# Short node tile moved as 112 rows and one, chunk bounds by TensorE transposes, pair table only in the general path, ScalarE normalises four tiles

## The chip, the cores and the metric

One core of one Trainium2 chip runs the whole program. The metric is the device time of one execution in microseconds, lower is better; the number to forecast is the median of the runs of the changed kernel.

## The reference

Two graph blocks over 625 nodes of 1024 features and 20,000 edges, each followed by a residual and a layer norm. Per edge there are `src`, `dst` (sorted) and a type of 2 and one of 8.

```python
x = _layernorm(x + _L0_gnn_ref(x, edge_index, edge_type_2, ...), axis=-1)
x = _layernorm(x + _L1_gnn_ref(x, edge_index, edge_type_8, ...), axis=-1)
# L0: norm_x = ln_weight * x * rsqrt(mean(x^2) + 1e-6)
#     y = elu(norm_x @ W_root + bias + sum_r mean over edges of type r of (norm_x[src] @ W_rel[r]))
#     returns x + y @ wo_weight
# L1: u = x @ root + bias + sum_r mean_r(x[src]) @ weight[r]          (8 types)
#     z = concat([u, x]) @ w_gate + b_gate;  returns tanh(u) * z + x * (1 - z)
```

## The kernel before

The program is written by hand for each engine (`block.sync`, `gpsimd`, `scalar`, `tensor`, `vector`), and semaphores order the engines among each other: each engine runs its own list from top to bottom, and a wait holds back all that stands behind it. Nodes lie on partitions in NT = 5 tiles of 128 rows; the last has TAIL = 113 real rows and 15 of zeros.

**Loading.** SyncE (SP) issues all DMAs. It loads the four edge lists, the norm weight, four full tiles of x in one DMA (L384) and, after the zeros are in place (`x_padded`), the 113 rows (L386). `x_loaded` of 32 means both have landed. It releases ScalarE's first work, the squares of `x` (L496), and SP's loads of the first weights (L396).

**Edge windows.** The mean over edges is done by matmuls with count matrices. The edges lie in 160 chunks of 125; nodes in 45 windows of 14 (`NWIN`). For each window VectorE finds the chunks that touch it, makes one-hot matrices of five chunks (`onehot_few`, L1319 and L1322), TensorE multiplies them (`count_few`, L837) and ScalarE copies the counts out (`copy_few`, L572 and L573). If a window ever needs more than MEET = 5 chunks, all three engines take a general path (`onehot_any` and its partners), which needs a table of pairs; with these inputs the short path runs. Which chunks touch a window comes from a bound for each of 80 partitions (L1209 to L1214), the maximum over the partitions by GpSimd (`partition_all_reduce`, L472, semaphore `bounds_max`), and a chain of twelve small VectorE instructions (L1225 to L1237) that makes the table and `most`, the largest number of chunks. All engines wait for that (`table_ready`).

**Order of VectorE in the first stage.** Windows 0 and 1, then the reciprocal of the RMS deviation (L1366, waits for ScalarE's `std`, L499), windows 2 and 3, splits of the transposed x (L1245), windows to 8, then the scale of the first weights, which waits for GpSimd's second `partition_all_reduce` (L482). That one waits for the absolute sums of the weights by ScalarE (`w0_sums`, L607). ScalarE normalises x (L611, `norm_x`) and TensorE transposes it (L826, `turn`) in between.

**GpSimd.** It clears x's last tile, makes the identity matrix (`ident`: a memset and an affine_select, L447 to L449) and the index constants (`consts_ready`, 12 in all), then runs the reductions above and one for each later weight unit.

**The last stage.** For tile t VectorE takes tanh(u) minus x, and for each half adds the gate product (L1760), multiplies (L1762), adds to x (L1763) and takes statistics (L1473). After the first half of tile t it normalises tile t - 1 in place (`norm_apply`: a reciprocal, L1481, and the 128x1024 subtract and multiply, L1485); ScalarE gives the deviation (L688), and SP stores tile t - 1 (L440). The last tile is normalised at the very end and its 113 rows are stored. SP then waits for all stores (L84).

```python
sp.wait_ge(x_padded, 1)
sp.dma_start(x[0:TAIL, NT - 1, :], x_d[(NT - 1) * P:NODES, :]).then_inc(x_loaded, 16)

pool.wait_ge(bounds_ready, 1)
nc.gpsimd.partition_all_reduce(wtmp[:, 10:12, :]..., wtmp[:, 8:10, :]..., CP, RMAX).then_inc(bounds_max, 1)

pool.wait_ge(w0_sums, DC)
pool.sem_inc(pool_turns, 1)
nc.gpsimd.partition_all_reduce(ar0[:, :], am0[:, :], P, RMAX).then_inc(max_ready, 1)
```

Of the kernel before, what the change touches and what calls it, by code (L numbers as in the profile page):

```python
# [5 lines left out]
ALU = mybir.AluOpType  # L6
ACT = mybir.ActivationFunctionType
AX = mybir.AxisListType
# [8 lines left out]
NPAD = NT * P  # L17
TAIL = NODES - (NT - 1) * P
DC = D // P
HALF = D // 2  # L20
# [61 lines left out]
def build(nc, x_d, src_d, dst_d, t2_d, t8_d, lnw_d, wrel_d, wroot_d, cb_d, wo_d,  # L82
          w1_d, root_d, b1_d, wg_d, bg_d, out_d):
    with ExitStack() as ctx:  # L84
        def sb(name, shape, dt):
            return ctx.enter_context(nc.sbuf_tensor(name, shape, dt))
# [4 lines left out]
        def sem(name):  # L91
            return ctx.enter_context(nc.semaphore(name))
# [18 lines left out]
        table = sb("table", [1, NWIN, 5], I32)  # L111

        most = sb("most", [1, 1], I32)
        rcnt0 = sb("rcnt0", [P, R0, NT], F32)
# [97 lines left out]
        keyT_ready = sem("keyT_ready")  # L212
        bounds_ready = sem("bounds_ready")
        bounds_max = sem("bounds_max")
        table_ready = sem("table_ready")
        onehot_free = sem("onehot_free")
# [78 lines left out]
        z_done = sem("z_done")  # L295
        out_ready = sem("out_ready")
        out_stored = sem("out_stored")

# [81 lines left out]
        def _(sp):  # L380
# [4 lines left out]
            sp.wait_ge(x_padded, 1)  # L385
            sp.dma_start(x[0:TAIL, NT - 1, :], x_d[(NT - 1) * P:NODES, :]).then_inc(x_loaded, 16)  # L386

# [3 lines left out]
            st0 = unit_weights(U_W0)[0]  # L391
            sp.wait_ge(x_loaded, 32)
            for a in range(2):
# [41 lines left out]
            for t in range(NT):  # L435
                sp.dma_start(x[:, t, :], x1_home[:, t, :]).then_inc(x1_back, 16)
            for t in range(NT):
                n = P if t < NT - 1 else TAIL
                sp.wait_ge(out_ready, t + 1)
                sp.dma_start(out_d[t * P:t * P + n, :], x[0:n, t, :]).then_inc(out_stored, 16)  # L440
            sp.wait_ge(out_stored, 16 * NT)


        @block.gpsimd
        def _(pool):
            nc.gpsimd.memset(x[:, NT - 1, :], 0.0).then_inc(x_padded, 1)
            nc.gpsimd.memset(ident[:, :], 0.0).then_inc(pool_steps, 1)  # L447
# [22 lines left out]

            pool.wait_ge(bounds_ready, 1)
            nc.gpsimd.partition_all_reduce(wtmp[:, 10:12, :].rearrange("p a j -> p (a j)"),  # L472
                                           wtmp[:, 8:10, :].rearrange("p a j -> p (a j)"), CP, RMAX).then_inc(bounds_max, 1)

            def unit_max(i, slot, parts=4):
# [16 lines left out]
        def _(act):  # L492
            act.wait_ge(x_loaded, 32)

# [90 lines left out]
            def copy_windows(j0, j1):  # L585

                with act.If(most_chunks <= MEET):
                    by_twos(act, j0, j1, copy_few)
                with act.Else():
                    by_twos(act, j0, j1, copy_any)  # L590

# [94 lines left out]
            def ln_deviation(k, t):  # L686
                act.wait_ge(ln_var[k], t + 1)
                nc.scalar.activation(std[:, 1 + k, t:t + 1], mv[:, k, t, 1:2], ACT.Sqrt, bias=eps[:, 1:2]).then_inc(ln_std[k], 1)  # L688
# [112 lines left out]
            for t in range(NT):  # L801
                if t + 2 < NT:
                    split_hi(2, t + 2, uT, 1.0)
                ln_deviation(1, t)


        @block.tensor
        def _(pe):
# [6 lines left out]
            last = nc.tensor.transpose(psC[:, 3 * CH:3 * CH + DC], lnw[:, :], ident[0:DC, 0:DC])  # L815
            last.then_inc(keys_turned, 1)

            def turn(k, t, src, ready):
# [43 lines left out]
            def count_windows(j0, j1):  # L862

                with pe.If(most_chunks <= MEET):
                    by_twos(pe, j0, j1, count_few)
                with pe.Else():
                    by_twos(pe, j0, j1, count_any)

# [299 lines left out]
        def _(dve):  # L1168
# [26 lines left out]


            dve.wait_ge(edges_loaded, 64)
            nc.vector.tensor_copy(ekey[:, 0, :, :], edges[:, 0, :, :]).then_inc(keys_ready, 1)
# [6 lines left out]
            step(ts(ctmp[:, 5, :], ctmp[:, 3, :], 16.0, None, ALU.mult))  # L1205
            dve.wait_ge(consts_ready, 12)
            base = win_base[0:CP, :]
            for h in range(2):
                step(ts(wtmp[:, h, :], base, ctmp[:, 5, h:h + 1], None, ALU.is_le))  # L1209
                step(stt(wtmp[:, 2 + h, :], base, ctmp[:, 4, h:h + 1], wtmp[:, h, :], ALU.is_ge, ALU.mult))  # L1210
                step(ts(wtmp[:, 4 + h, :], wtmp[:, 2 + h, :], ctmp[:, 0, h:h + 1], None, ALU.mult))
                step(ts(wtmp[:, 6 + h, :], wtmp[:, 2 + h, :], ctmp[:, 1, h:h + 1], None, ALU.mult))
            step(tt(wtmp[:, 8, :], wtmp[:, 4, :], wtmp[:, 5, :], ALU.max))
            tt(wtmp[:, 9, :], wtmp[:, 6, :], wtmp[:, 7, :], ALU.max).then_inc(bounds_ready, 1)  # L1214
            dve.wait_ge(keys_turned, 1)
# [3 lines left out]


            dve.wait_ge(bounds_max, 1)

            def row(a):
                return wtmp[0:1, a, :]
            step(ts(row(12), row(10), -1.0, 200.0, ALU.mult, ALU.add))  # L1225
            step(tt(row(13), row(11), row(12), ALU.subtract))
            pairs_i = wtmp[0:1, 14, :].bitcast(I32)
            step(ts(pairs_i, row(13), 0.5, 0.25, ALU.mult, ALU.add))
            step(ts(row(15), pairs_i, float(PAIRS), None, ALU.max))
            step(ts(row(16), row(15), -2.0, float(CH), ALU.mult, ALU.add))  # L1230
            step(nc.vector.tensor_tensor_scan(row(17), row(22), row(15), 0.0, ALU.mult, ALU.add))
            step(tt(table[:, :, 0], row(12), row(16), ALU.min))
            step(nc.vector.tensor_copy(table[:, :, 1], row(15)))
            step(tt(table[:, :, 2], row(17), row(15), ALU.subtract))
            step(nc.vector.tensor_copy(table[:, :, 3], row(17)))
            step(ts(table[:, :, 4], row(12), float(CH - MEET), None, ALU.min))
            nc.vector.tensor_reduce(most[:, :], row(13), AX.X, ALU.max).then_inc(table_ready, 1)  # L1237

            def split_lo(k, t, dst, gain):
# [67 lines left out]
            dve.wait_ge(table_ready, 1)  # L1307
            dve.wait_ge(keyT_ready, 1)
            most_chunks = dve.value_load(most[0:1, 0:1], min_val=1, max_val=CH)
            win8 = iota_win[0:EC, 0:WIN * R1]  # L1310
# [32 lines left out]
            def onehot_windows(j0, j1):  # L1343

                with dve.If(most_chunks <= MEET):
                    by_twos(dve, j0, j1, onehot_few)
                with dve.Else():
                    by_twos(dve, j0, j1, onehot_any)

# [400 lines left out]
            for t in range(NT):  # L1750
# [4 lines left out]
                for h in range(2):  # L1755
# [9 lines left out]
                    if t and h == 0:  # L1765
                        norm_apply(1, t - 1, out_ready)
                norm_var(1, t)
            norm_apply(1, NT - 1, out_ready)

# [22 lines left out]
```

## Time and profile before

| what | value |
|---|---|
| time, median of 3 runs (lowest to highest) | 974.63 us (973.67 to 975.96) |
| profiled execution, its own time | 975.7 us |
| its span | 973.8 us |
| TensorE busy / VectorE / ScalarE / GpSimd | 886.3 / 738.9 / 458.6 / 20.5 us |
| DMA | 63.43 MB, mean 65 GB/s |
| granted TensorE clock, mean | 0.97 |

The profile's page divides the span into 40 slices of 24.3 us. TensorE is busy for nine tenths of most slices from the fourth to the thirty-ninth; the first two and the last are the ones with room. The DMA engines move little after the start: the third slice has 3 GB/s and the second 178. The views used below are the timeline (start, duration, engine, line, operation, and in square brackets how long the engine was idle before it and what ended that), the chain of waits that ended last, busy time by stretch, the waits of SP, and the list of DMA issues.

### The profile page before, as it was taken

To read this page: it belongs to the slowest core of one execution; us is meant where nothing else is said; L and a number is where in the kernel's file an instruction comes from. 1 tells how busy PE (TensorE), PEld (TensorE's weight loads), DVE (VectorE), ACT (ScalarE), POOL (GpSimd) and SP (SyncE) were. 2 spreads that over 40 slices of the span, in tenths; PEclk is the share of its full clock that TensorE was granted. 3 is DMA by queue.
4 is the path that set the end of the run, shared out by engine and by line. 5 is a ranking of instruction groups with operands and counts; after the bars stand their busy time and mean duration, and the time that the engine had idled before them with its cause. 6 is when DMAs were issued, how large, how long until landed. Compare 5 with 4: busy or idle time off the path is not lost.

```text
span 973.8 us, 18919 instructions
## 1 busy us (share of the span) xinstructions
PE 886.3 (91%) x7115; PEld 648.0 (67%) x7116; DVE 738.9 (76%) x1216; ACT 458.6 (47%) x748; POOL 20.5 (2%) x46
## 2 busy tenths in 40 slices
PE   0568999898999899999999999999999999999980
PEld 0555887654458776787687787778778767876440
DVE  3589999496899777777777877776787777776891
ACT  0684445365465545535535453553544455338200
POOL 1000001000000000000000000000000000000000
PEclk9789999999999999999999999999999999999995
DMA  3501000251202222022022202202210220222011
GB/s 114 178 3 50 1 0 0 90 217 66 87 1 87 87 87 87 1 88 87 5 81 86 77 9 86 86 0 86 86 55 31 86 86 23 88 87 108 22 44 41
DMA packets 30343, 63.43 MB, mean 65 GB/s; under 512 B 1481, under 2 KB 4689, under 8 KB 30289
## 3 DMA queue, kind: packets, MB, share of 16 engines
q1 hardware_dynamic: 30289, 62.71, 18.2%
q8 instruction: 34, 0.56, 0.2%
q14 instruction: 20, 0.16, 0.1%
HBM read 57.52 MB, written 5.18 MB: 64 GB/s over the span
## 4 chain that ended last, share of the span: by engine, by line
PE 76%; DVE 12%; ACT 4%; DMA 3%; issue 2%; DVEq 0%; SPq 0%; POOL 0%; ACTq 0%; POOLq 0%
PE psP L1037 40%; PE psA L1107 18%; PE psP L837 6%; PE psP L886 4%; PE psA L875 4%; DMA x<-in_x 3%; DVE wsplit L1279 2%; PE psP L962 1%; DVE wsplit L1273 1%; PE psA L826 1%; DVE stats L1473 1%; DVE u_mem L1518 1%; DVE wsplit L1393 1%; ACT u_mem L607 1%; ACT wsplit L548 1%
## 5 line engine op out<-in xcount | busy, mean ns | idle before, releaser
L1037 PE MATMUL psP<-wsplit,xT 128*128 128x256 f16 x2592 | 296.4, 273 | 3.2 <-ACT vec L734 2.8
L1037 PEld LDWEIGHTS psP<-wsplit,xT 128*128 128x128 f16 x2592 | 254.3, 98 | 37.5 <-issue 3.1
L1107 PE MATMUL psA<-p_mem,c_mem 128*128 128x512 f16 x800 | 175.3, 379 | 0.0
L1037 PE MATMUL psP<-wsplit,x 128*128 128x256 f16 x1296 | 150.3, 273 | 1.7 <-DVE key_mem L1584 1.5
L1107 PEld LDWEIGHTS psA<-p_mem,c_mem 128*128 (+1 forms) x800 | 78.4, 98 | 90.9
L1037 PEld LDWEIGHTS psP<-wsplit,x 128*128 128x128 f16 x1296 | 126.6, 98 | 16.8 <-issue 2.2
L1279 DVE SCALAR_TENSOR_TENSOR wsplit<-stage,sc,wsplit 128x1024 f16<-128x1024 f32 x90 | 114.8, 1279 | 26.5 <-ACT wsplit L559 26.5
L559 ACT ACTIVATE wsplit<-stage,sc 128x1024 f16<-128x1024 f32 x90 | 100.6, 1137 | 15.0 <-DVE sc L1184 9.1
L837 PE MATMUL psP<-p_mem 125*128 125x140 f16 x1125 | 79.1, 234 | 22.7 <-DVE p_mem L1322 18.2
L837 PEld LDWEIGHTS psP<-p_mem 125*128 125x128 f16 x1125 | 76.2, 103 | 27.0 <-issue 14.9
L1549 DVE SCALAR_TENSOR_TENSOR u_mem<-psA,coef,u_mem 128x512 f32<-128x512 f32 x80 | 60.0, 750 | 32.9 <-PE psA L1107 30.9
L559 ACT ACTIVATE wsplit<-x,sc 128x1024 f16<-128x1024 f32 x54 | 61.7, 1143 | 39.2 <-PE psP L1037 32.6
L1279 DVE SCALAR_TENSOR_TENSOR wsplit<-x,sc,wsplit 128x1024 f16<-128x1024 f32 x54 | 69.2, 1282 | 10.3 <-ACT wsplit L559 10.2
L538 ACT ACTIVATE key_mem<-stage 128x1024 f16<-128x1024 f32 x72 | 75.8, 1053 | 1.7
L1322 DVE TENSOR_SCALAR p_mem<-iota_src,key_mem 125x640 f16<-125x640 f16 x225 | 70.4, 382 | 0.0
L572 ACT ACTIVATE c_mem<-psP 128x336 f32 (+1 forms) x90 | 36.8, 411 | 42.8 <-PE psP L837 42.8
L886 PE MATMUL psP<-wsplit,xT 128*128 128x512 f16 x240 | 54.3, 387 | 1.0 <-DVE u_mem L1518 1.0
L886 PE MATMUL psP<-wsplit,c_mem 128*128 128x512 f16 x240 | 52.5, 379 | 1.7 <-DVE wsplit L1273 1.7
L734 ACT ACTIVATE vec<-psP 128x512 f32<-128x512 f32 x16 | 9.5, 594 | 93.2 <-PE psP L1037 93.2
L1319 DVE SCALAR_TENSOR_TENSOR p_mem<-iota_win,win_base,key_mem 125x560 f16<-125x560 f16 x90 | 48.3, 579 | 5.7 <-issue 2.7
L875 PE MATMUL psA<-wsplit,xT 128*128 128x429 f16 x240 | 48.6, 353 | 3.5 <-issue 2.4
L1565 DVE SCALAR_TENSOR_TENSOR p_mem<-psP,p_mem 128x512 f16<-128x512 f32 x32 | 22.1, 692 | 32.2 <-ACT p_mem L731 32.2
(201 smaller groups left out, 804.8 us busy)
## 6 DMA issues: line engine op xcount, KB each, us to landing
stage<-in_L_gnn_weight SPq DMA_DIRECT2D x16, 2048.0 KB, 8.0
stage<-in_L_gnn_w_gate SPq DMA_DIRECT2D x4, 2048.0 KB, 7.9
x_home<-x SPq DMA_DIRECT2D x5, 512.0 KB, 2.6
x<-x_home SPq DMA_DIRECT2D x5, 512.0 KB, 5.5
stage<-in_L_gnn_W_rel SPq DMA_DIRECT2D x4, 572.0 KB, 8.6
x<-in_x SPq DMA_DIRECT2D x1, 2048.0 KB
xT<-in_L_gnn_root SPq DMA_DIRECT2D x1, 2048.0 KB, 7.9
stage<-in_L_gnn_root SPq DMA_DIRECT2D x1, 2048.0 KB, 8.1
```

Source lines behind the costliest of these rows:

```text
L538: nc.scalar.activation(land, st[:, part], ACT.Abs, accum_out=am[:, slot, n:n + 1]).then_inc(wsum_ready, 1)
L559: nc.scalar.activation(split_block(n, 0), step_block(REL, slot, n), ACT.Copy, scale=sc_f[:, scale_col(REL, slot), 2:3]).then_inc(whi_ready, 1)
L572: nc.scalar.activation(o8, w8, ACT.Copy)
L837: last = nc.tensor.matmul(psP[:, 2 * b + s // 3, col:col + WCOLS], src[:, s * P:(s + 1) * P], win, start=(first and s % 3 == 0), stop=Fals ...
L875: last = nc.tensor.matmul(out, lhs[:, a, c, bass.ts(t, P)], w[:, c, cols], start=first, stop=(c == chunks - 1 and a == 1))
L886: last = nc.tensor.matmul(out, lhs[:, a, c, bass.ts(t, P)], wsplit[:, s:s + 2, b, cols], start=first, stop=(c == DC - 1 and a == 1))
L1037: last = nc.tensor.matmul(psP[:, bank, (col + tt) * FB:(col + tt + 1) * FB], lhs[tt](a, c), split_block(n, b)[:, c, :], start=(first and t ...
L1107: last = nc.tensor.matmul(psA[:, (NT * h + t) % 2, :], cnt8[:, r, s, t * P:(t + 1) * P], p_part[h][a][:, s, :], start=(s == 0 and a == 0), ...
L1279: stt(split_block(n, 1), step_block(REL, slot, n), sc_f[:, scale_col(REL, slot), 2:3], split_block(n, 0), ALU.mult, ALU.subtract).then_inc ...
L1319: stt(oh_win[:, b, :, cols], w.unsqueeze(1).broadcast_to([EC, MEET, n]), wb, keyT[:, bass.ds(chunk, MEET), a:a + 1].broadcast_to([EC, MEET ...
L1322: ts(oh_src[:, b, k, :], iota_src[0:EC, :], keyT[:, chunk + k, 0:1], None, ALU.is_equal).then_inc(chunk_ready, 1)
L1549: stt(uv, psA[:, (NT * h + t) % 2, :], coef[:, t:t + 1], uv, ALU.mult, ALU.add).then_inc(agg_done, 1)
```

## The change

- The last tile of x is loaded, and stored, as two DMAs: rows 0 to 111 and row 112. `x_loaded` now counts to 48, and the last stores wait for a semaphore of their own, `last_ready`.
- The zeros of x's last tile are written by VectorE, no longer by GpSimd.
- The bounds are made by six instructions over both halves at once plus one maximum, behind four of the constants and not twelve. The maximum over partitions is a TensorE transpose, a VectorE maximum, and a second transpose; GpSimd's `partition_all_reduce` for it is gone.
- Of the twelve instructions of the table four remain (read straight from PSUM); the other eight are run only in the general path (`pair_table`).
- In the last stage ScalarE normalises tiles 0 to 3, with `shift` and `rstd` from VectorE; VectorE still does tile 4.

```diff
+EVEN = TAIL // 16 * 16
 # sync
-            sp.dma_start(x[0:TAIL, NT - 1, :], x_d[(NT - 1) * P:NODES, :]).then_inc(x_loaded, 16)
+            for r0, r1 in ((0, EVEN), (EVEN, TAIL)):
+                sp.dma_start(x[r0:r1, NT - 1, :], x_d[(NT - 1) * P + r0:(NT - 1) * P + r1, :]).then_inc(x_loaded, 16)
...
-            sp.wait_ge(x_loaded, 32)
+            sp.wait_ge(x_loaded, 48)
...
-            for t in range(NT):
-                n = P if t < NT - 1 else TAIL
+            for t in range(NT - 1):
                 sp.wait_ge(out_ready, t + 1)
-                sp.dma_start(out_d[t * P:t * P + n, :], x[0:n, t, :]).then_inc(out_stored, 16)
-            sp.wait_ge(out_stored, 16 * NT)
+                sp.dma_start(out_d[t * P:(t + 1) * P, :], x[:, t, :]).then_inc(out_stored, 16)
+            sp.wait_ge(last_ready, 1)
+            for r0, r1 in ((0, EVEN), (EVEN, TAIL)):
+                sp.dma_start(out_d[(NT - 1) * P + r0:(NT - 1) * P + r1, :], x[r0:r1, NT - 1, :]).then_inc(out_stored, 16)
+            sp.wait_ge(out_stored, 16 * (NT + 1))
 # gpsimd
-            nc.gpsimd.memset(x[:, NT - 1, :], 0.0).then_inc(x_padded, 1)
...
-            pool.wait_ge(bounds_ready, 1)
-            nc.gpsimd.partition_all_reduce(wtmp[:, 10:12, :].rearrange("p a j -> p (a j)"),
-                                           wtmp[:, 8:10, :].rearrange("p a j -> p (a j)"), CP, RMAX).then_inc(bounds_max, 1)
 # scalar, last stage, t from 0 to 4
+                if t:
+                    act.wait_ge(out_factors, 2 * t)
+                    nc.scalar.activation(x[:, t - 1, :], x[:, t - 1, :], ACT.Identity, bias=shift[:, t - 1:t],
+                                         scale=rstd[:, 2, t - 1:t]).then_inc(out_ready, 1)
                 ln_deviation(1, t)
 # tensor, behind the transposes of the keys
+            pe.wait_ge(bounds_ready, 1)
+            nc.tensor.transpose(psA[0:2 * NWIN, 0, 0:CP], wtmp[:, 8:10, :].rearrange("p a j -> p (a j)"),
+                                ident[0:CP, 0:CP]).then_inc(bounds_turned, 1)
+            pe.wait_ge(bounds_top, 1)
+            nc.tensor.transpose(psA[0:1, 1, 0:2 * NWIN], btop[:, :], ident[0:2 * NWIN, 0:2 * NWIN]).then_inc(bounds_max, 1)
 # vector
+            nc.vector.memset(x[:, NT - 1, :], 0.0).then_inc(x_padded, 1)
...
-            dve.wait_ge(consts_ready, 12)
-            base = win_base[0:CP, :]
-            for h in range(2):
-                step(ts(wtmp[:, h, :], base, ctmp[:, 5, h:h + 1], None, ALU.is_le))
...
+            dve.wait_ge(consts_ready, 4)
+            base = win_base[0:CP, :].unsqueeze(1).broadcast_to([CP, 2, NWIN])
...
+            step(tt(wtmp[:, 0:2, :], base, by_half(5), ALU.is_le))
...
+            tt(wtmp[:, 8:10, :], ends[:, 0, :, :], ends[:, 1, :, :], ALU.max).then_inc(bounds_ready, 1)
             dve.wait_ge(keys_turned, 1)
...
+            dve.wait_ge(bounds_turned, 1)
+            nc.vector.tensor_reduce(btop[:, :], psA[0:2 * NWIN, 0, 0:CP], AX.X, ALU.max).then_inc(bounds_top, 1)
             dve.wait_ge(bounds_max, 1)
...
+            low, high = psA[0:1, 1, 0:NWIN], psA[0:1, 1, NWIN:2 * NWIN]
+            step(ts(row(12), low, -1.0, 200.0, ALU.mult, ALU.add))
+            step(tt(row(13), high, row(12), ALU.subtract))
+            ts(table[:, :, 4], row(12), float(CH - MEET), None, ALU.min)
             nc.vector.tensor_reduce(most[:, :], row(13), AX.X, ALU.max).then_inc(table_ready, 1)
...
 # vector, last stage
                     if t and h == 0:
-                        norm_apply(1, t - 1, out_ready)
+                        norm_reciprocal(1, t - 1).then_inc(out_factors, 1)
+                        dve.wait_ge(out_factors, 2 * t - 1)
+                        ts(shift[:, t - 1:t], mv[:, 1, t - 1, 0:1], rstd[:, 2, t - 1:t], -1.0,
+                           ALU.mult, ALU.mult).then_inc(out_factors, 1)
                 norm_var(1, t)
-            norm_apply(1, NT - 1, out_ready)
+            norm_apply(1, NT - 1, last_ready)
```

The order of instructions is shown at two places. First GpSimd behind its constants, before the change (`ISA` is an instruction of GpSimd's own set; one with operands here is a `partition_all_reduce`, the bare one ahead of the first of them is added when the program is built):

```order
L468 MEMSET c_mem 128x40x10
L469 MEMSET u_mem 128x10x10
L472 ISA
L472 ISA u_mem<-u_mem 80x90 [waits bounds_ready]
L482 ISA ar<-am 128x8 [waits w0_sums]
```

and in the changed program:

```order
L477 MEMSET c_mem 128x40x10
L478 MEMSET u_mem 128x10x10
L487 ISA [waits w0_sums]
L487 ISA ar<-am 128x8
L489 MEMSET stage 128x1024 [waits w0_lo]
```

The reduction of the bounds is gone, and the bare instruction that stood in front of it, ahead of the wait for `bounds_ready`, now stands in front of the reduction of the weights' sums, behind the wait for `w0_sums`.

Second, VectorE in the last stage between the two halves of a tile, before:

```order
L1473 BN_STATS stats<-x 128x6 [waits dve_steps]
L1481 RECIPROCAL rstd<-std 128x1 [waits ln_var1,ln_std1,dve_steps]
L1485 TENSOR_SCALAR x<-x,mv,rstd 128x1024 [waits dve_steps]
L1760 SCALAR_TENSOR_TENSOR p_mem<-psP,cz,p_mem 128x512 [waits z_full]
L1762 TENSOR_TENSOR p_mem<-p_mem,u_mem 128x512 [waits z_done]
```

and now:

```order
L1508 BN_STATS stats<-x 128x6 [waits dve_steps]
L1516 RECIPROCAL rstd<-std 128x1 [waits ln_var1,ln_std1,dve_steps]
L1803 TENSOR_SCALAR shift<-mv,rstd 128x1 [waits out_factors]
L1795 SCALAR_TENSOR_TENSOR p_mem<-psP,cz,p_mem 128x512 [waits z_full]
L1797 TENSOR_TENSOR p_mem<-p_mem,u_mem 128x512 [waits z_done]
```

A 128x1024 instruction has given way to one of 128x1; the wide one stands on ScalarE, ahead of its deviation of the next tile.

## Rows read from the trace of the kernel before

**Rows 1.** The page: busy time, share of the span and instructions of each engine.
```profile
PE 886.3 (91%) x7115; PEld 648.0 (67%) x7116; DVE 738.9 (76%) x1216; ACT 458.6 (47%) x748; POOL 20.5 (2%) x46
```
**Rows 2.** The chain that ended last, start: start us, us, what.
```profile
3.53 25.02 DMA x<-in_x
```
**Rows 3.** Busy time by stretch: stretch, us, engines (instructions), clock, DMA share, GB/s.
```profile
6.00:10.00 4.00, 0.53 (x3) 0.53 (x3) 0.28 (x2) 0.00 (x0) 0.86 (x5) 1.00 1.02 412
10.30:28.40 18.10, 3.30 (x26) 3.09 (x26) 9.55 (x35) 0.00 (x0) 1.94 (x11) 1.00 0.06 26
```
**Rows 4.** Timeline, 0 to 36 us, all engines.
```profile
0.74 0.95 POOL L446 MEMSET x<- 128x1024 f32 x1 [0.29 <-POOLq L1782]
...
9.13 0.28 POOL L449 TENSOR_SCALAR_AFFINE_SELECT ident<-ident 128x128 f32<-128x128 f32 x1 [7.30 <-issue]
...
9.47 1.55 PE L813 MATMUL psC<-ident,u_mem 80*125 80x80 f32 x6 [9.47 <-POOL ident L449]
...
9.64 0.12 POOL L456 IOTA u_mem<- 80x2 f32 x1
...
11.43 0.17 POOL L469 MEMSET u_mem<- 128x100 f16 x1
...
13.91 0.20 DVE L1214 TENSOR_TENSOR u_mem<-u_mem 80x45 f32<-80x45 f32 x1
...
19.00 0.63 POOL L472 PARTITION_ALL_REDUCE u_mem<-u_mem  x1 [7.40 <-issue]
...
22.23 0.19 DVE L1237 TENSOR_REDUCE most<-u_mem 1x1 int32<-1x45 f32 x1
24.50 1.07 DVE L1319 SCALAR_TENSOR_TENSOR p_mem<-iota_win,win_base,key_mem 125x560 f16<-125x560 f16 x2 [2.08 <-issue]
...
26.02 5.50 PE L837 MATMUL psP<-p_mem 125*128 125x140 f16 x50 [14.80 <-DVE p_mem L1322]
...
28.58 1.06 ACT L496 ACTIVATE wsplit<-x 128x1024 f32<-128x1024 f32 x1 [26.55 <-DMA x<-in_x]
...
35.53 0.19 DVE L1366 RECIPROCAL rstd<-std 128x5 f32<-128x5 f32 x1 [6.00 <-ACT std L499]
```
**Rows 5.** Timeline, 36 to 75 us, TensorE, GpSimd and VectorE.
```profile
37.40 1.97 PE L826 MATMUL psA<-ident,wsplit 128*128 128x128 f32 x8 [5.89 <-ACT wsplit L611]
...
43.88 5.14 PE L837 MATMUL psP<-p_mem 125*128 125x140 f16 x50
...
48.86 1.04 PE L826 MATMUL psA<-ident,wsplit 128*128 128x128 f32 x8
...
64.55 1.18 POOL L482 PARTITION_ALL_REDUCE ar<-am  x1 [44.91 <-ACT u_mem L607]
...
68.75 1.08 DVE L1319 SCALAR_TENSOR_TENSOR p_mem<-iota_win,win_base,key_mem 125x560 f16<-125x560 f16 x2 [0.86 <-PE psP L837]
```
**Rows 6.** Timeline, 925 to 974 us, last stage.
```profile
925.64 20.88 PE L886 MATMUL psP<-wsplit,c_mem 128*128 128x512 f16 x96
...
931.46 0.16 DVE L1481 RECIPROCAL rstd<-std 128x1 f32<-128x1 f32 x1
...
932.39 0.75 DVE L1760 SCALAR_TENSOR_TENSOR p_mem<-psP,cz,p_mem 128x512 f32<-128x512 f32 x1
...
948.76 0.75 DVE L1760 SCALAR_TENSOR_TENSOR p_mem<-psP,cz,p_mem 128x512 f32<-128x512 f32 x1
...
952.49 0.81 DVE L1485 TENSOR_SCALAR x<-x,mv,rstd 128x1024 f32<-128x1024 f32 x1
```
**Rows 7.** Timeline, 210 us, VectorE, factors of the first layer norm.
```profile
210.13 0.16 DVE L1481 RECIPROCAL rstd<-std 128x1 f32<-128x1 f32 x1 [0.38 <-ACT std L688]
...
210.46 0.55 DVE L1454 TENSOR_TENSOR p_mem<-psA,p_mem 128x384 f16<-128x384 f32 x1
```
**Rows 8.** SP's waits (us in total, times, longest), and a DMA issue (KB, us to landing).
```profile
SPq L84 <- DMA out<-x: 19.8, 1, 19.8
...
x_home<-x SPq DMA_DIRECT2D x5, 512.0 KB, 2.6
```

More of the change, by code:

```diff
@@ L111, in build @@
         table = sb("table", [1, NWIN, 5], I32)
+        btop = sb("btop", [2 * NWIN, 1], F32)
         most = sb("most", [1, 1], I32)
@@ L213, in build @@
         bounds_ready = sem("bounds_ready")
+        bounds_turned = sem("bounds_turned")
+        bounds_top = sem("bounds_top")
         bounds_max = sem("bounds_max")
+        pairs_ready = sem("pairs_ready")
         table_ready = sem("table_ready")
@@ L296, in build @@
         out_ready = sem("out_ready")
+        out_factors = sem("out_factors")
+        last_ready = sem("last_ready")
         out_stored = sem("out_stored")
@@ L492, in _ @@
         def _(act):
-            act.wait_ge(x_loaded, 32)
+            act.wait_ge(x_loaded, 48)
             for t in range(NT):
@@ L589, in copy_windows @@
                 with act.Else():
+                    if j0 == 0:
+                        act.wait_ge(pairs_ready, 8)
                     by_twos(act, j0, j1, copy_any)
@@ L866, in count_windows @@
                 with pe.Else():
+                    if j0 == 0:
+                        pe.wait_ge(pairs_ready, 8)
                     by_twos(pe, j0, j1, count_any)
@@ L1205, in _, with by_half @@
             step(ts(ctmp[:, 5, :], ctmp[:, 3, :], 16.0, None, ALU.mult))
-            dve.wait_ge(consts_ready, 12)
-            base = win_base[0:CP, :]
-            for h in range(2):
-                step(ts(wtmp[:, h, :], base, ctmp[:, 5, h:h + 1], None, ALU.is_le))
[L1210 to L1214, printed above, removed]
+            dve.wait_ge(consts_ready, 4)
+            base = win_base[0:CP, :].unsqueeze(1).broadcast_to([CP, 2, NWIN])
+            def by_half(a):
+                return ctmp[:, a, :].unsqueeze(2).broadcast_to([CP, 2, NWIN])
+            step(tt(wtmp[:, 0:2, :], base, by_half(5), ALU.is_le))
+            step(tt(wtmp[:, 2:4, :], base, by_half(4), ALU.is_ge))
+            step(tt(wtmp[:, 0:2, :], wtmp[:, 0:2, :], wtmp[:, 2:4, :], ALU.mult))
+            step(tt(wtmp[:, 4:6, :], wtmp[:, 0:2, :], by_half(0), ALU.mult))
+            step(tt(wtmp[:, 6:8, :], wtmp[:, 0:2, :], by_half(1), ALU.mult))
+            ends = wtmp[:, 4:8, :].rearrange("p (a h) j -> p h a j", h=2)
+            tt(wtmp[:, 8:10, :], ends[:, 0, :, :], ends[:, 1, :, :], ALU.max).then_inc(bounds_ready, 1)
             dve.wait_ge(keys_turned, 1)
@@ L1224, in row, with pair_table @@
                 return wtmp[0:1, a, :]
[L1225 to L1236, printed above, removed]
-            nc.vector.tensor_reduce(most[:, :], row(13), AX.X, ALU.max).then_inc(table_ready, 1)
+            low, high = psA[0:1, 1, 0:NWIN], psA[0:1, 1, NWIN:2 * NWIN]
+            step(ts(row(12), low, -1.0, 200.0, ALU.mult, ALU.add))
+            step(tt(row(13), high, row(12), ALU.subtract))
+            ts(table[:, :, 4], row(12), float(CH - MEET), None, ALU.min)
+            nc.vector.tensor_reduce(most[:, :], row(13), AX.X, ALU.max).then_inc(table_ready, 1)
+            def pair_table():
+                pairs_i = wtmp[0:1, 14, :].bitcast(I32)
+                chain = (lambda: ts(pairs_i, row(13), 0.5, 0.25, ALU.mult, ALU.add),
+                         lambda: ts(row(15), pairs_i, float(PAIRS), None, ALU.max),
+                         lambda: ts(row(16), row(15), -2.0, float(CH), ALU.mult, ALU.add),
+                         lambda: nc.vector.tensor_tensor_scan(row(17), row(22), row(15), 0.0, ALU.mult, ALU.add),
+                         lambda: tt(table[:, :, 0], row(12), row(16), ALU.min),
+                         lambda: nc.vector.tensor_copy(table[:, :, 1], row(15)),
+                         lambda: tt(table[:, :, 2], row(17), row(15), ALU.subtract),
+                         lambda: nc.vector.tensor_copy(table[:, :, 3], row(17)))
+                for n, op in enumerate(chain):
+                    op().then_inc(pairs_ready, 1)
+                    dve.wait_ge(pairs_ready, n + 1)
             def split_lo(k, t, dst, gain):
@@ L1308, in _ @@
             dve.wait_ge(keyT_ready, 1)
+            dve.wait_ge(consts_ready, 12)
             most_chunks = dve.value_load(most[0:1, 0:1], min_val=1, max_val=CH)
@@ L1347, in onehot_windows @@
                 with dve.Else():
+                    if j0 == 0:
+                        pair_table()
                     by_twos(dve, j0, j1, onehot_any)
```

## Prediction

> **What bounds the kernel now.** I read the page first, then the chain of waits, then the timeline at both ends. TensorE is busy for 886.3 of 973.8 us [rows 1], so nearly all that a change can take away lies where TensorE idles: at the start and at the end. The long middle is touched by nothing here; it can only be shifted.
>
> At the start the chain of waits has one piece of 25.02 us, the DMA of x that was issued at 3.53 and landed at 28.55 [rows 2]. That is the short tile: 113 rows, 452 KB. The stretches say how it went. From 6 to 10 us the DMA engines are full at 412 GB/s; from 10.3 to 28.4 us their share is 0.06, one engine in sixteen, at 26 GB/s [rows 3]. So the four full tiles are there by 10.3 us, and the 113 rows crawl over one engine. ScalarE's squares start at 28.58, and its deviation releases VectorE's reciprocal at 35.53 [rows 4].
>
> A second chain runs beside it. GpSimd's constants end at 11.60, the bounds end at 14.11, the reduction over partitions starts only at 19.00, the table is ready at 22.42, the first one-hot starts at 24.50 [rows 4]. It is hidden behind the DMA: VectorE has windows 0 and 1 done at 29.53 and waits 6.00 us for `std`. It will not be hidden once the DMA is short.
>
> At the end VectorE's last instruction ends at 953.30 [rows 6], and SP then waits 19.8 us for the store of the 113 rows [rows 8], where a store of 128 rows and 512 KB lands 2.6 us after its issue [rows 8].
>
> **1. Load of 112 rows and one.** If 112 rows spread over all engines, 452 KB at 412 GB/s add 1.1 us to the four tiles' 10.3, and ScalarE begins at about 11.5 in place of 28.58: 17.1 us earlier, `std` at about 18.4. SP issues one DMA more, behind transfers that take until 11; it hides. VectorE's memset of x (GpSimd took 0.95 [rows 4]) lies before VectorE has edges to work on and costs nothing; without that cover it would cost that 0.95.
>
> **2. The table.** GpSimd loses its first memset, so the affine_select can start at about 8.2, not 9.13, and the fourth constant, which ended at 9.76, is there at 8.85 [rows 4]. (If the 7.30 us idle before it count from elsewhere, 0.9 us of this is lost.) The seven bounds instructions are twice as wide as the old ones. The old twelve of the table took from 19.63 to 22.42, 0.23 us each [rows 4]; I take 0.28: until 10.8. The key transposes took 1.75 us with the one of the norm weight and end at about 10.3. A transpose is 0.26 (1.55 for six) [rows 4]: the bounds are turned at 11.1, but VectorE copies the keys until 11.5. Then maximum, transpose and four small instructions: 0.25 + 0.3 + 4 x 0.23, table at about 13.0, 9.4 us earlier than 22.42. The 2.08 us of register loads and branch behind it stay; the eight other constants end before it. First one-hot at 15.1, windows 0 and 1 done at 20.1.
>
> **1 and 2 together.** The reciprocal needs both: `std` (18.4) and VectorE (20.1). The table is now the later one, so the front moves from 35.53 to 20.1, by 15.4; ScalarE, which used to make up its copies of windows 0 and 1 behind `std`, now has one of them behind it, and I take **15.6 us**. Either part alone would give about 6 (the x load) or nothing (the table).
>
> **3. TensorE's clock.** From 31.5 to 37.4 TensorE idled, and eight transposes then took 1.97 us, at a granted 0.50 (1.2 GHz), against 1.04 at 48.86 at full clock; the 50 matmuls at 43.88 took 5.14 [rows 5]. Now the transposes follow on the 50 matmuls at once, with a gap of some 3 us behind them. If the clock stays at 2.4 GHz, up to 2.8 us go (0.9 of a transpose batch, 1.9 of the 50 matmuls); but the step below adds an idle stretch and slow matmuls behind it, up to 1.5 us. I take **0.7 gained**, ends +2.8 and -1.5.
>
> **4. The bare GpSimd instruction.** This one runs against the change. Twice in the trace GpSimd idles for no semaphore: 7.30 us between the memset of `ident` and the affine_select, and 7.40 us between L469 (ends 11.60) and the first reduction [rows 4]. Both times such a bare instruction stands in between; it changes what GpSimd can run. Before the change the second lay ahead of the wait for `bounds_ready`, and 2.5 of its 7.4 us were over when the bounds came (14.11). Now it lies behind `w0_sums`. The old reduction there started at once behind ScalarE's last sum, at 64.55 [rows 5], and VectorE, ScalarE (`w0_scaled`) and through them TensorE waited for it. So the reduction comes about 7.35 later. Against that, VectorE used to wait 0.86 us at 68.75 for a window's counts [rows 5], which will long be there: 0.8 back. Cost **6.6 us**. Bounds: 4.9 from 14.11 to 19.00, if loading began only with the wait, to 7.4.
>
> The Trainium skill, page GPSIMD Engine Reference, section 2.1, states about 6 us for the first call to a freshly loaded kernel, with no visible instruction. By that rule step 4 would cost 1.4 less and the time would be 944.3; the two rows of this trace show 7.3 and 7.4.
>
> **5. Normalising on ScalarE.** A reciprocal at 931.46 and the next half at 932.39: 0.93 us a tile [rows 6]. With `shift` instead, the same pair in the first layer norm takes 0.33, from 210.13 to 210.46 [rows 7]. That is 0.60 for each of tiles 1 to 3; tile 0's falls where TensorE is the bound, until 925.6. **1.8 us.** TensorE does not take it back: it ends at 946.52, and the last half's first instruction moves from 948.76 to 946.96 [rows 6], 0.4 later. ScalarE's 1.1 us or so for a 128x1024 tile [rows 4] end long before the deviation that stands behind each. Were it late, VectorE's next reciprocal would wait.
>
> **6. Last store.** From VectorE's end at 953.30 to the span's end at 973.8 are 20.5 us, 19.8 of them SP's wait [rows 8]; the other 0.7 are the issue and the program's end, which stay. Now the wait is for two stores: the large one is bounded by the 2.6 us of 128 rows, of which the second issue (some 0.35) hides a part; the row adds its own issue. I take 2.4 of wait. **17.4 us.**
>
> **Sum.** 15.6 + 0.7 - 6.6 + 1.8 + 17.4 = 28.9. Against the profiled execution's 975.7 that is 946.8. That execution is 1.1 above the median of 974.63, so the forecast is **945.7 us**.
>
> **Rivals.**
> (a) *The loading is free*: GpSimd has done it before the sums come. Then VectorE waits as before: 945.7 - 6.6 = 939.1. For it: 45 us of idle GpSimd lie ahead of L482. Against: the instruction stands behind the wait in the changed order. Chance 0.06.
> (b) *Slower, the 112 rows still go over one engine.* Place: both moves of the last tile. Then x lands at 28.6 as before, the earlier table gains nothing, the end keeps its 20 us, and what is left is the loading on the weights' path: 974.63 + 6.6 - 1.8 + 0.4 (one more issue) = 979.8. It decides if the bytes move at 26 GB/s and not at 400; the whole turns slower once the two moves, with the table behind the first, give less than 6.6 + 0.4 - 1.8 = 5.2 us. For it: 112 is closer to 113 than to 128, and no row shows a DMA of 112. Against: the 128-row stores do spread. Chance 0.03. The Trainium skill, page DMA: Bandwidth & Descriptors, section on why a DMA increments its semaphore by 16, says that a DMA uses the largest number up to 16 that divides its outermost dimension: one engine for 113, sixteen for 112. By that rule (b) is out; the rows bear out its half on 113.
> (c) *The front gives part back*: with everything 15 us earlier another engine's order is the bound between 20 and 50 us, or the clock stays low through the stage after the stall. A loss of 5 to 9: 951 to 955. For it: copies, splits, one-hots and sums of three engines follow closely on each other there. Against: all their predecessors move by the same amount, and the first weights, 3.4 MB released by x, need 8.4 us at 412 GB/s and are there by 21. Chance 0.11.
>
> **How the numbers follow.** Forecast 0.80, (a) 0.06, (b) 0.03, (c) 0.11. The unknowns of the forecast, load of the code -2.5 or +0.1, clock -2.1 or +2.2, the affine_select +0.9, the store and landing one either way, reach from 940 to 950; taking in the near edge of (c) the range is 940 to 951. A measurement can tell about 0.2%, 2 us. Only (b) is slower: 0.03; same 0.01; faster 0.96.
>
> **What would show it.** Right: squares near 11.5, `most` near 13, reciprocal near 20; GpSimd's first reduction preceded by some 7 us of idle and VectorE's wait there of 7 (step 4); L1803 where L1485 was, at 0.33 a tile; last store landed within 3 us. Wrong: squares still after 28 (b); a reduction right behind `w0_sums` (a); a reciprocal at 20 but `w0_sums` less than 12 earlier than 64.5 (c).

## The result, and the profile after

The changed kernel takes 945.49 us (median of 4 runs, 943.75 to 946.21) against 974.54 us for the kernel before (973.67 to 975.96). The ratio is 0.9698, 95% interval 0.968 to 0.9716: faster by 3.0%, 29.05 us between the medians. The profiled execution took 945.65 us, its span is 943.8. The forecast was 945.7, range 940 to 951.

The page of the changed kernel, span and busy time, then TensorE and the DMA rate in 40 slices of 23.6 us:

```profile
span 943.8 us, 18917 instructions
...
PE 884.8 (94%) x7117; PEld 646.1 (68%) x7118; DVE 734.1 (78%) x1206; ACT 463.5 (49%) x752; POOL 18.2 (2%) x44
...
PE   3659999899998999999999999999999999999996
...
GB/s 264 40 2 51 1 0 1 98 217 68 90 1 90 90 90 89 2 91 90 0 89 89 0 89 89 12 77 89 47 41 89 84 5 90 112 2 90 112 23 87
```

TensorE has the same work as in [rows 1] (884.8 us for 886.3) in a span 30.0 us shorter; all but 1.5 us of what went was idle time. The x load, and the first weights that it releases, now lie within the first slice (264 GB/s), and in the last slice TensorE is busy for six tenths.

The timeline of the changed kernel, 0 to 60 us (start, duration, engine, line, operation; in brackets the idle time before it and what ended that):

```profile
8.85 0.28 POOL L458 TENSOR_SCALAR_AFFINE_SELECT ident<-ident 128x128 f32<-128x128 f32 x1 [7.90 <-issue]
...
12.92 1.06 ACT L501 ACTIVATE wsplit<-x 128x1024 f32<-128x1024 f32 x1 [10.90 <-DMA x<-in_x]
...
13.08 0.18 DVE L1255 TENSOR_REDUCE most<-u_mem 1x1 int32<-1x45 f32 x1
...
15.30 1.07 DVE L1352 SCALAR_TENSOR_TENSOR p_mem<-iota_win,win_base,key_mem 125x560 f16<-125x560 f16 x2 [2.04 <-issue]
...
19.54 0.30 ACT L504 ACTIVATE std<-ss,eps 128x5 f32<-128x5 f32 x1
...
20.24 0.18 DVE L1401 RECIPROCAL rstd<-std 128x5 f32<-128x5 f32 x1
...
28.23 3.96 PE L853 MATMUL psP<-p_mem 125*128 125x140 f16 x50
...
32.03 1.04 PE L842 MATMUL psA<-ident,wsplit 128*128 128x128 f32 x8
...
47.30 0.20 ACT L614 ACTIVATION_READ_ACCUMULATOR u_mem<-stage,lnwT 128x1 f32 x1
...
53.73 0.39 POOL L487 PARTITION_ALL_REDUCE ar<-am  x1 [42.41 <-issue]
54.23 0.16 DVE L1412 TENSOR_REDUCE ar<-ar 128x1 f32<-128x8 f32 x1 [4.74 <-POOL ar L487]
...
57.15 1.07 DVE L1352 SCALAR_TENSOR_TENSOR p_mem<-iota_win,win_base,key_mem 125x560 f16<-125x560 f16 x2 [0.87 <-DVE convb L1421]
```

Two more lines bear on the stall. The first is from the kernel before, the last of ScalarE's sums of the weights; the second is GpSimd's memset behind its reduction in the changed kernel:

```profile
64.14 0.20 ACT L607 ACTIVATION_READ_ACCUMULATOR u_mem<-stage,lnwT 128x1 f32 x1
```

```profile
70.42 0.95 POOL L489 MEMSET stage<- 128x1024 f32 x1 [16.30 <-DVE wsplit L1428]
```

Read against [rows 4, 5], the timeline is a ledger of how far ahead of the old kernel the new one is at each mark. Squares: 12.92 for 28.58. Reciprocal: 20.24 for 35.53, 15.3 ahead. The eight transposes behind the 50 matmuls: 32.03 for 48.86, 16.8 ahead; the 50 matmuls took 3.96 us and not 5.14, because TensorE's clock rose to its upper level earlier on the way through: the granted clock was 0.56 from 28.23 to 30.00 us and 1.00 from 30.00 to 32.10, against 0.50 from 43.88 to 46.00 and 0.68 from 46.00 to 49.00 in the kernel before. Then GpSimd: the last sum ends at 47.50 and the reduction starts at 53.73, with no semaphore named for the idle time before it. That idle time, ahead of the first instruction of another kind, is what the text below calls the fetch of GpSimd's code. From the last sum to VectorE's next window are 9.65 us, where the old kernel took 4.4 (its last sum ended at 64.34, the window of [rows 5] is at 68.75). So the lead falls to 68.75 - 57.15 = 11.6 us.

The chain of waits of the changed kernel has the same 6 us as its longest piece of the first 75 us apart from the wait for GpSimd's code at the very start:

```profile
47.96 5.77 issue
53.73 0.40 POOL ar L487
```

The last stage of the changed kernel, timeline from 908 us:

```profile
909.25 0.21 DVE L1803 TENSOR_SCALAR shift<-mv,rstd 128x1 f32<-128x1 f32 x1
909.38 0.74 DVE L1795 SCALAR_TENSOR_TENSOR p_mem<-psP,cz,p_mem 128x512 f32<-128x512 f32 x1
909.50 1.24 ACT L813 ACTIVATE x<-x,shift,rstd 128x1024 f32<-128x1024 f32 x1 [5.42 <-DVE shift L1803]
...
914.47 20.88 PE L904 MATMUL psP<-wsplit,c_mem 128*128 128x512 f16 x96
...
935.78 0.74 DVE L1795 SCALAR_TENSOR_TENSOR p_mem<-psP,cz,p_mem 128x512 f32<-128x512 f32 x1
...
939.50 0.81 DVE L1520 TENSOR_SCALAR x<-x,mv,rstd 128x1024 f32<-128x1024 f32 x1
```

and SP's waits (us in total, times, longest):

```profile
SPq L404 <- DMA x<-in_x: 8.6, 1, 8.6
...
SPq L85 <- DMA out<-x: 2.4, 1, 2.4
```

TensorE's last 96 products start at 914.47 where [rows 6] has 925.64: 11.2 ahead, so of the lead of 11.6 us only 0.4 was lost in the 857 us between. GpSimd's reductions place that loss between 147 and 189 us (42.26 us between two of them, 41.82 in the kernel before), where nothing was changed; the same stretch took from 41.8 to 42.7 us over all ten kernels. VectorE's last half is at 935.78 for 948.76: 13.0 ahead, 1.8 of it won in this stage. And SP waits 2.4 us for the last store where it waited 19.8 [rows 8]; with one more issue the end of the span is 30.0 ahead.

### The profile page after: what moved, and what is told of

The parts are those of the page before. It is cut to its first block, busy times and chain, and to the rows that moved or that the text cites. A ratio compares the mean times of both kernels' runs of the same rounds, so it can differ in the third digit from the quotient of the medians.

```text
span 943.8 us, 18917 instructions
## 1 busy us (share of the span) xinstructions
PE 884.8 (94%) x7117; PEld 646.1 (68%) x7118; DVE 734.1 (78%) x1206; ACT 463.5 (49%) x752; POOL 18.2 (2%) x44
## 4 chain that ended last, share of the span: by engine, by line
PE 78%; DVE 13%; issue 4%; ACT 4%; DVEq 1%; POOL 0%; POOLq 0%; ACTq 0%
PE psP L1055 41%; PE psA L1125 18%; PE psP L853 6%; PE psP L904 5%; PE psA L893 4%; DVE wsplit L1311 2%; PE psP L980 1%; DVE wsplit L1305 1%; PE psA L842 1%; DVE stats L1508 1%; DVE u_mem L1553 1%; DVE p_mem L1355 1%; DVE wsplit L1428 1%; ACT u_mem L614 1%; ACT wsplit L553 1%
## 5 line engine op out<-in xcount | busy, mean ns | idle before, releaser
L1055 PEld LDWEIGHTS psP<-wsplit,x 128*128 128x128 f16 x1296 | 126.7, 98 | 16.8 <-issue 2.2
L577 ACT ACTIVATE c_mem<-psP 128x336 f32 (+1 forms) x90 | 36.9, 412 | 42.3 <-PE psP L853 42.3
```

The costliest lines, as they stand in the source:

```text
L577: nc.scalar.activation(o8, w8, ACT.Copy)
L1055: last = nc.tensor.matmul(psP[:, bank, (col + tt) * FB:(col + tt + 1) * FB], lhs[tt](a, c), split_block(n, b)[:, c, :], start=(first and t ...
```

## The experiments

Eight kernels ran. The theory to test was the forecast's own: three gains (load, table, store), one smaller (normalising), and one price, code that GpSimd fetches behind `w0_sums`. Its rivals were that the stall belongs to the sums or the reduction, and that an early table or load is worth its full length alone.

**The price, moved out of the way.** `e1_early_load` adds a reduction that nobody reads (its spare tile and its semaphore are left out here):

```diff
             nc.gpsimd.memset(cnt2[:, :, :, NPAD - WPAD:NPAD], 0.0).then_inc(counts_padded, 1)
+            pool.wait_ge(consts_ready, 12)
+            nc.gpsimd.partition_all_reduce(spare[:, :], eps[:, 0:1], P, RMAX).then_inc(early_max, 1)
```

> The changed kernel with one more partition_all_reduce on GpSimd (one column of a constant into a spare tile, read by nobody) right behind its constants, so that the bare instruction and its some 6 us of idle fall at 11 to 19 us, where nobody waits. Theory of the code load: GpSimd's reduction starts within 0.3 us of ScalarE's last sum, VectorE's wait there falls from 4.7 us to under 1, and the time from 945.5 to about 940.3 (5.2 less). Rival, the stall behind w0_sums belongs to the reduction or to the sums themselves: the wait stays and the time is 945.5 within 1 us.

Measured: 939.34 us (938.11 to 941.77), ratio to the kernel before 0.9637, interval 0.9621 to 0.9653, which does not touch the changed kernel's. Its timeline, 17 to 53 us:

```profile
17.46 0.64 POOL L483 PARTITION_ALL_REDUCE spare<-eps  x1 [5.93 <-issue]
...
47.54 0.63 POOL L492 PARTITION_ALL_REDUCE ar<-am  x1 [29.43 <-ACT u_mem L619]
...
49.23 0.15 DVE L1417 TENSOR_REDUCE ar<-ar 128x1 f32<-128x8 f32 x1
...
52.15 1.07 DVE L1357 SCALAR_TENSOR_TENSOR p_mem<-iota_win,win_base,key_mem 125x560 f16<-125x560 f16 x2 [0.87 <-PE psP L858]
```

The 5.93 us of idle now stand in front of the idle reduction; the real one starts as soon as the sums are there, and VectorE does not wait for it. The window is at 52.15 for 57.15: 5.0 us, where 5.2 were expected. The profiled spans differ by 6.3; 1.3 of that, net, is gained behind 147 us, and lies in a dip of TensorE's clock near 213 us that the profiled execution of the changed kernel has and this one has not (last section). The medians differ by 6.15. Whether the other executions of the changed kernel have the dip isn't shown; their mean granted clocks (0.979 to 0.981, against 0.980 to 0.989 here) fit it. This kernel beats both.

**The price, doubled.** `e7_two_code_loads` has, on top of that, one instruction of the other kind behind the wait:

```diff
             pool.wait_ge(w0_sums, DC)
             pool.sem_inc(pool_turns, 1)
+            nc.gpsimd.iota(back[:, :], pattern=[[1, 8]], base=0, **loose).then_inc(early_max, 1)
             nc.gpsimd.partition_all_reduce(ar0[:, :], am0[:, :], P, RMAX).then_inc(max_ready, 1)
```

> The kernel with the early reduction (e1_early_load), and one small iota put behind the wait for the weights' sums, ahead of the reduction; its result goes to a spare tile and nobody reads it. Theory, GpSimd holds the code for either kind of instruction and each change loads it again: two loads of some 6.1 us each on the path, the reduction starts 12 us behind the last sum: 939.3 + 12.2 = 951.5. Rival, code once loaded stays: 939.3.

Measured: 952.41 us (952.29 to 953.66), 13.1 more than `e1_early_load` and 0.9 more than expected. GpSimd in its timeline, the sums ending at 46.90:

```profile
54.08 0.14 POOL L493 IOTA back<- 128x8 f32 x1 [36.85 <-issue]
60.36 0.39 POOL L494 PARTITION_ALL_REDUCE ar<-am  x1 [6.14 <-issue]
60.85 0.16 DVE L1419 TENSOR_REDUCE ar<-ar 128x1 f32<-128x8 f32 x1 [11.99 <-POOL ar L494]
```

Two fetches, 7.2 and 6.14 us, one for each change of kind, though both codes had been fetched once before. So it is the change of kind that costs, each time anew. The kinds are the iota and affine_select on one side and the reduction on the other; a memset runs in either state. The changed kernel's memset at 70.42 stands behind its reduction and starts 0.05 us after VectorE releases it.

**The load alone.** `e2_x_load_only` is the kernel before with the first hunk of the diff:

```diff
-            sp.dma_start(x[0:TAIL, NT - 1, :], x_d[(NT - 1) * P:NODES, :]).then_inc(x_loaded, 16)
+            for r0, r1 in ((0, EVEN), (EVEN, TAIL)):
+                sp.dma_start(x[r0:r1, NT - 1, :], x_d[(NT - 1) * P + r0:(NT - 1) * P + r1, :]).then_inc(x_loaded, 16)
```

> The kernel before with the load of the short tile as 112 rows and one, and nothing else. Forecast's theory: x lands near 13, the deviation is ready near 20, but VectorE is busy with the one-hots of the late table until 29.5, so the reciprocal moves from 35.53 to 29.6 only: 5.9 less, with up to 1.2 more because TensorE no longer idles before the transposes: 967.5 to 968.7. Rival, the load alone gives the whole front: 974.5 - 15.3 = 959.2. Rival, 112 rows do not spread: 974.5.

Measured: 966.30 us (964.96 to 968.46), ratio 0.9916, interval 0.9898 to 0.9934: 8.3 less, a gain 1.2 us larger than the upper end of what was expected (7.1). The mechanism holds, the load does not bring the whole front; most of the surplus is in its timeline, 17 to 29 us:

```profile
17.99 0.63 POOL L474 PARTITION_ALL_REDUCE u_mem<-u_mem  x1 [6.05 <-issue]
...
20.03 0.30 ACT L501 ACTIVATE std<-ss,eps 128x5 f32<-128x5 f32 x1
...
21.20 0.19 DVE L1239 TENSOR_REDUCE most<-u_mem 1x1 int32<-1x45 f32 x1
...
28.42 0.18 DVE L1368 RECIPROCAL rstd<-std 128x5 f32<-128x5 f32 x1
```

The deviation is ready at 20.33 and VectorE takes the reciprocal only at 28.42, behind its one-hots: the table is the bound. But the table itself came 1.0 us earlier than in [rows 4] (21.20 for 22.23), since GpSimd's fetch took 6.05 us and not 7.40, although nothing was changed on that chain. The only difference in the program is that no 113-row transfer runs beside it; seven traces in all bear this out (last section).

**The bounds alone.** `e4_bounds_only` is the changed kernel with its load, store, normalising and memset of x put back as before.

> The kernel before with the bounds, the transposes for their maximum and the short table of the change, and nothing else (load, store, normalising and the memset of x as before). Theory: the table is ready near 14, but x lands at 28.6 as before and hides it; the code load moves behind the sums of the weights and costs 5.2: slower, 979.7. Rival, an earlier table is worth something by itself: 974.5 or less.

Measured: 980.07 us (978.64 to 980.89), ratio 1.0048, interval 1.0032 to 1.0063: slower by 5.5. In its timeline VectorE has the windows done long before it gets the deviation, and later waits for the fetch:

```profile
13.69 0.18 DVE L1248 TENSOR_REDUCE most<-u_mem 1x1 int32<-1x45 f32 x1
...
35.40 0.19 DVE L1394 RECIPROCAL rstd<-std 128x5 f32<-128x5 f32 x1 [14.46 <-ACT std L502]
...
70.04 0.40 POOL L485 PARTITION_ALL_REDUCE ar<-am  x1 [58.12 <-issue]
70.54 0.16 DVE L1405 TENSOR_REDUCE ar<-ar 128x1 f32<-128x8 f32 x1 [5.26 <-POOL ar L485]
```

The same edit that is part of a gain of 29 us is a loss of 5.5 by itself: its 8.5 us in front (13.69 for 22.23) are hidden behind the x load, its price is not.

**The change without the bounds.** `e8_without_bounds` is the kernel before with load, store and normalising of the change.

> The change without its part on the bounds and the table (load, store and normalising as changed; bounds, reduction on GpSimd, table of twelve and the memset of x as before). Theory, the parts add up once x is short: 966.3 (load alone) - 16.3 (store alone) - 1.8 (normalising alone) = 948.2, so the bounds as made are worth some 2.7 of the change (8 gained in front, 5 to 6 given back to the code load). Rival, the bounds are worth nothing or less also here: 945.5 or below.

Measured: 947.39 us (946.56 to 947.82), ratio 0.9712, interval 0.9699 to 0.9725 (its runs of the kernel before had a median of 975.43). Against the changed kernel's 0.9698 the bounds would be worth 1.4 to 1.9 us as they were made; with the fetch out of the way (`e1_early_load`, 0.9637) they are worth 7 to 8. The intervals of this kernel and of the changed one overlap by half, so by the times alone the smaller worth isn't shown. The traces show more: behind the fetch VectorE's window is at 59.96 us here and at 57.15 in the changed kernel, 2.8 apart (2.7 were expected), and the reductions near 147 us are still 2.8 apart. At the end 1.5 is left, because the profiled execution of the changed kernel has the dip of the clock near 213 us and this one has not.

**The store alone**, and **the normalising alone**, each the kernel before with that hunk of the diff:

> The kernel before with the store of the short tile as 112 rows and one, and nothing else. Theory: SP's last wait falls from 19.8 to 2.4 us with one issue more, 17.0 less: 957.5. Rival, part of the 17 us at the end came from the other parts of the change: 960 or more.

> The kernel before with tiles 0 to 3 normalised by ScalarE and nothing else. Theory: three of the four pairs lie where VectorE is the bound, 0.60 us each: 972.8 (1.8 less). Rival, TensorE's last products take it back: 974.6.

Measured: 958.31 us (957.71 to 958.71), ratio 0.9827, 16.3 less, for the store; its last wait is 2.4 us as in the changed kernel. 972.73 us (972.07 to 974.27), ratio 0.9983, interval 0.9974 to 0.9992, 1.8 less, for the normalising. The normalising is as expected; the store's gain is 0.8 short of the expected 17.0, within what its runs and those of the kernel before scatter.

**The rows of a DMA.** `e6_split_56_57` changes one number, and with it both moves of the short tile:

```diff
-EVEN = TAIL // 16 * 16
+EVEN = 56
```

> The changed kernel with the short tile cut into 56 and 57 rows (both moves). Theory, a DMA uses the largest number of engines up to 16 that divides its rows: 14 for 56, 3 for 57, so 228 KB at 3 x 26 GB/s = 2.9 us: SP's last wait 4 us in place of 2.4, the load hardly later than VectorE's table: 947 to 948. Rival, only multiples of 16 rows spread and others go over one engine: both pieces crawl, the last wait is again about 20 us and x lands near 28: 970. Rival, only the count of 113 is special: 945.5.

Measured: 950.55 us (2 runs, 949.67 and 951.43). Busy time by stretch, behind the four tiles and during the last store (stretch, us, engines, clock, DMA share, GB/s), and SP's last wait:

```profile
12.00:14.00 2.00, 0.31 (x1) 0.08 (x1) 0.89 (x7) 0.00 (x0) 0.00 (x0) 1.00 0.19 78
945.00:946.50 1.50, 0.00 (x0) 0.00 (x0) 0.00 (x0) 0.00 (x0) 0.00 (x0) 0.50 0.20 82
```

```profile
SPq L85 <- DMA out<-x: 5.3, 1, 5.3
```

A share of 0.19 is three engines of sixteen, and 82 GB/s is about three times the 26 of [rows 3]. The 57 rows went over three engines, which is the largest number up to 16 that divides 57; 113 rows went over one. Neither rival fits. The time was missed all the same: 947 to 948 were expected, and 950.55 is 2.6 more (two executions, 1.8 apart; the profiled one, at 949.67, is 1.7 more). Two terms were too small. The wait is 5.3 us, not 4; that the 56 rows take a part of those three engines first would explain it, and was not tried. And the squares start at 14.73, so that the deviation, no longer the table, is the bound: the reciprocal is at 21.68 for 20.24, 1.4 us later, where next to nothing was expected. The rule of the Trainium skill (DMA: Bandwidth & Descriptors, section on why a DMA increments its semaphore by 16) holds for 57 and 113 rows here, and 112 rows at a share of 0.8 to 1.0 fit its sixteen (1.00 from 941.5 to 942.0 us, in the changed kernel's last store).

## Why the prediction was right, and where not

The median was forecast at 945.7 and is 945.49. That is closer than the working deserves, and the last microsecond is luck: the sum was 28.9 us against the profiled executions, and these are 30.05 apart (975.7 to 945.65). The forecast then took off another 1.1, by which the old profiled execution lay above its median, as if the new one would lie as far above its own; it lies 0.16 above. The two errors cancel. Term by term, from the ledger above:

| step | forecast | measured |
|---|---|---|
| 1 and 2, front by window 2 | 15.6 | 15.6 (36.38 to 20.73) |
| 3, clock | +0.7 | +1.2 |
| 4, code fetch | -6.6 | -5.2 |
| 5, normalising | +1.8 | +1.8 |
| 6, last store | +17.4 | +17.0 |
| in no step: between 147 and 189 us | 0 | -0.4 |
| sum | 28.9 | 30.0 |

**Step 1** had the x load 1.4 us too early: squares at 12.92, not 11.5. The short tile's bytes did not flow at 412 GB/s:

```profile
10.50:12.25 1.75, 0.86 (x5) 0.41 (x4) 1.56 (x6) 0.00 (x0) 0.82 (x8) 1.00 0.81 192
```

The engines are 0.81 busy and move 192 GB/s. It cost nothing, because the table was the bound, as the forecast had said: deviation at 19.84, VectorE at 20.24.

**Step 2** was right in sum (13.26 for 13.0) and wrong in one part. Taking the memset away was to bring the affine_select 0.95 us forward and brought 0.28 (8.85 for 9.13). Over all ten kernels it starts at 9.01 to 9.70 with the memset ahead of it and at 8.48 to 9.06 without, 0.5 apart on average: about half of the 0.95, between the forecast and its bracket. The instructions between made up for most of it; the bounds are six instructions, not the seven that the description of the change and the forecast count.

**Step 4** is the term that was mis-sized, 5.2 us for 6.6, in three parts. The fetch took 6.2 us and not 7.35: of the two rows it was taken from, one lay at the program's start and one beside the 113-row transfer. The Trainium skill's figure (GPSIMD Engine Reference, section 2.1, about 6 us) was nearer than those rows, and the forecast should have asked what else ran beside them. Second, the 0.8 us that VectorE was to get back does not exist: [rows 5] names TensorE for the 0.86 us before the window at 68.75, but in the changed kernel the counts are long done and the same 0.87 us stand there, now put down to VectorE itself. So the wait was not for counts, and the releaser named was merely the last semaphore; the register loads that stand ahead of a window's one-hots in the kernel are the likely cause, and were not tried. Third, the reduction itself was quicker by 0.8 (0.39 for 1.18). That the price exists, where it falls and that it is paid in full is shown by `e1_early_load` and `e7_two_code_loads`.

**Steps 3, 5 and 6** stand. In step 3 the first eight transposes ran at a granted 1.00 as forecast (1.09 us for 1.97); the 50 matmuls gained 1.2 of the 1.9, and the 1.5 kept for slow matmuls behind the stall did not appear as a loss of lead. In step 5 a reciprocal and the next half are 0.33 us apart (935.45 and 935.78), as forecast. `e1_early_load` at 939.34 is also what rival (a) forecast for a fetch that costs nothing (939.1). Rival (b), 112 rows over one engine, is out by the 2.4 us wait and `e6_split_56_57`. Rival (c), the front gives part back, did not come: the lead grew to 16.8 by 32 us, and up to the window at 57.15 only the fetch took from it.

## What to carry to other kernels

A DMA whose row count has no large divisor up to 16 may be by far the slowest thing at the start or end of a program: look for a stretch in which the DMA share is one sixteenth, and cut the rows into a multiple of 16 and a rest. When an engine's first use of some facility is removed, ask what its next use has to do first; here the order of instructions showed 5 us that the diff did not, and one reduction on GpSimd in its idle time took them back. And of two chains in parallel neither brings the whole alone: the load alone gave 8.3 us and the bounds alone cost 5.5, while both, with the fetch out of the way, put VectorE's window 16.6 us earlier (52.15 for 68.75).

## What the runs showed of the hardware

GpSimd's fetch of code is not of one length. Ahead of the first reduction, idle time was 7.40 us in the kernel before, 7.62 in `e3_store_only` and 7.18 in `e5_norm_only`, all with the 113-row transfer running beside it; it was 6.05, 5.93, 5.84 and 5.84 us in `e2_x_load_only`, `e1_early_load`, `e7_two_code_loads` and `e8_without_bounds`, where x had landed by 12.6 to 13.4 us, early in the fetch. The kernel before and `e2_x_load_only` differ in that transfer alone. So a transfer that crawls over one engine goes with a fetch over 1 us longer, in one profiled execution of each of seven kernels; by what path they meet was not tried. A busy DMA as such does not do it: from 14 to 18 us of `e2_x_load_only` the share is 0.70 and then 1.08, and the fetch is one of the short ones. Behind `w0_sums`, with the DMA nearly idle, it took 6.0 to 6.6 us (6.2 in the changed kernel). Back to the iota it took 7.2 us, with no transfer beside it, so the length may also depend on the kind that is fetched.

The fetch recurs at every change of kind (`e7_two_code_loads`). That code is moved in this time is not seen in the traces: the queues for instructions carry the same 0.56 and 0.16 MB in all ten, and the DMA share from 54.20 to 60.30 us of `e7_two_code_loads` is 0.00. What they show is the idle time, where it stands, and what brings it on.

TensorE's clock can fall in one execution and not in another at the same place of the same work. Changed kernel first, then `e1_early_load`, the same work 4.66 us earlier:

```profile
211.00:213.00 2.00, 0.39 (x2) 0.00 (x0) 1.57 (x6) 0.79 (x2) 0.00 (x0) 1.00 0.00 0
213.00:215.00 2.00, 1.78 (x10) 1.24 (x11) 1.97 (x4) 1.79 (x3) 0.00 (x0) 0.77 0.22 88
215.00:217.00 2.00, 2.00 (x6) 0.71 (x5) 1.71 (x4) 0.31 (x2) 0.00 (x0) 0.50 0.43 174
```

```profile
206.34:208.34 2.00, 0.39 (x2) 0.00 (x0) 1.57 (x6) 0.78 (x2) 0.00 (x0) 1.00 0.00 0
208.00:210.00 2.00, 1.44 (x11) 1.10 (x12) 1.97 (x4) 1.81 (x3) 0.00 (x0) 1.00 0.04 16
210.00:212.00 2.00, 2.00 (x11) 0.94 (x10) 1.90 (x4) 0.37 (x1) 0.00 (x0) 1.00 0.61 246
```

The granted clock falls to 0.50 (1.2 GHz) in the first and stays at 1.00 (2.4 GHz) in the second, though TensorE was busy for the same 0.39 us in the same 2 us ahead of it; six matmuls run where eleven do at 1.00. Between the same two reductions of GpSimd lie 38.27 us in the first (188.94 to 227.21) and 36.59 in the second (184.28 to 220.87). Over the ten profiled executions it is one or the other: 38.27 in the kernel before, the changed one, `e4_bounds_only`, `e5_norm_only` and `e6_split_56_57`, and 36.58 or 36.59 in the other five. The kernel before, `e3_store_only` and `e5_norm_only` run the same program up to the last stage, and the dip is in the first and the last of them and not in the second. So it comes and goes with no edit ahead of it; what decides it is open. The five with the dip had been 0.1 to 0.9 us quicker over the stretch before (41.8 to 42.3 us between two reductions, against 42.4 to 42.7), so the net cost is 1.2 us on average. Executions of one kernel differ by some 2.5 us here; how much of that is the dip isn't known, as one execution of each was profiled.
